# A two-layer conv and expert kernel: the layer norms shared by ScalarE and GpSimd, with new instruction orders

## The chip, the cores and the metric

The kernel runs on one core of a Trainium2 chip. A core has TensorE (PE in the profile; PEld is its weight load), VectorE (DVE), ScalarE (ACT), GpSimd (POOL) and SyncE (SP), each with its own instruction stream, held together by semaphores. The metric is the device time in microseconds of one execution; the median of three runs is given.

## The reference, cut to what matters

The input is x of 16 x 16 x 8 x 64 (height, width, image, channel). Two layers follow one another, and each has a convolution-like half and an expert half, both with a layer norm in front and a residual behind:

```
x = x + L0_conv(ln(x, 1e-6))      # projections, gates, four linear scans, norm, projection
t = x as 8 x 256 tokens
t = t + L0_ffn(ln(t, 1e-5))       # 16 experts, silu(h1) * h2, the two best weighted
x = x + L1_conv(ln(x, 1e-6))
t = t + L1_ffn(ln(t, 1e-5))       # 8 experts, gelu, the two best weighted
ln(v, eps) = (v - mean(v)) / sqrt(var(v) + eps)      # over the 64 channels
```

What is touched here is `ln` alone: two norms a layer, each over all 2048 rows of 64 channels.

## The kernel before

The rows lie in SBUF as 16 tiles of 128 rows by 64 channels. The work is cut into nine units (`UNITS`): in layer 0 two of one image (two tiles, 256 columns) and three of two images (four tiles, 512 columns), in layer 1 four of two images. Each unit goes through the same stages, and the stages of several units overlap.

A norm exists twice per unit, "a" ahead of the conv half and "e" (the token norm) ahead of the experts, so there are 18: 4 of two tiles, 14 of four. Each runs: DVE takes statistics (`a0`/`e0`), aggregates them (`a1`/`e1`) and adds eps (`a2`/`e2`, tile `spread`); POOL raises that to the power -0.5 (`ra`/`re`, tile `rstd`) and then subtracts the mean and multiplies by `rstd`, one `tensor_scalar` instruction for each tile (`an`/`en`, L599); PE transposes two tiles at a time (`TA`/`TE`, L1152); ACT and DVE split the result into a high and a low part (`za`/`al` and `ze`/`el`, tiles `conv_z` and `tok_z`), which the products read.

In the expert half PE makes two up products per expert (`U`, L1148 and L1149), ACT applies silu (`si`) or gelu (`ga`, `gb`), in layer 0 DVE multiplies (`hd`), PE makes the down product of two experts (`D`, L1263), DVE weighs it with the gates (`wp`), and POOL adds it up (`ad`, L664). The gates of a unit come from DVE and POOL (`sh`, ending in tile `gates`), are turned on PE, written to DRAM by ACT's queue and read back by SP's queue, broadcast to all partitions (`gates_b`).

The order on each engine is written out by hand, in five tables of short names (`PE_ORDER`, `DVE_ORDER`, `ACT_ORDER`, `POOL_ORDER`, `SP_ORDER`). An engine executes its table strictly in order; an instruction that waits for a semaphore holds all behind it. In `PE_ORDER` a name carries the PSUM bank and what must have freed it.

`NORM_BY` says which engine makes a unit's norm ("P" is POOL). Code for "S" (ACT) and "V" (DVE) is there and not used before; the "S" form is `Identity(rstd * x + shift)` with `shift = -mean * rstd`, for which DVE makes `minus_mean` (L948) and POOL the product (L588).

Of the kernel before, what the change touches and what calls it, by code (L numbers as in the profile page):

```python
# [4 lines left out]
H, W, B, D = 16, 16, 8, 64  # L5
# [23 lines left out]
NORM_BY = {"a": "PPPPPPPPP", "e": "PPPPPPPPP"}  # L29
# [19 lines left out]
D:3hd54 D:5al5 I:4wp23 F:2si55 XT:0si56 U:1hd55:6y4 U:7hd56:3wp24 U:5wp25:1si57 U:6hd57:7si58 TE:0x2 D:3hd58
U:5si59:1hd59 LG:6si60 U:0el4:7hd60 mx:5si61 U:3wp26:6lg4 D:1hd61 U:0si62:3si63 U:7hd62:6hd63 U:5mc1:1wp27  # L50
GT:0si64 D:7si65 D:5si66 D:0gt4 D:3hd64 U:2sc5:4sc5 TA:7wp28 O:5wp29 U:2si67:6hd65 U:1hd66:4hd67 GB:5og5 I:2si68
U:1si69:7al6 U:0wp30:6hd68 F:4hd69 U:1si70:3wp31 D:7hd70 D:0si71 D:5y5 D:1si72 XT:6hd71 U:3hd72:7wp32
U:0wp33:5wp34 U:3si73:1wp35 U:6x3:0si74 TE:7hd73 U:3si75:5hd74 U:1hd75:6si76 D:3si77 D:1si78 U:0hd76:5hd77
U:7el5:3wp36 LG:0si79 D:1wp37 U:6hd78:0lg5 O:7ga0 U:3gb0:6ga1 TA:0gb1 U:2sc6:4sc6 D:5hd79 I:3ga2 F:1wp38
U:6gb2:0al7 GB:2ga3 XT:4gb3 U:5wp39:7og6 GT:0gb4 O:6ga4 U:4x4:5ga5 U:7gb5:0gt5 D:2y6 D:4ga6 TE:7ga7 TA:5gb6
D:0gb7 LG:1sc7 U:3sc7:7el6 U:5al8:1lg6 U:3ga8:2wp40 U:7gb8:5ga9 GB:1gb9 I:6og7 U:3ga10:4wp41 F:2gb10 GT:5gb11
D:0wp42 D:7ga11 D:5gt6 U:3ga12:1y7 U:4gb12:0wp43 O:3ga13 TE:1gb13 D:4ga14 U:2sc8:6sc8 U:0gb14:1el7 U:7wp44:2ga15
LG:5wp45 GB:6gb15 U:0ga16:3og8 U:7ga17:1gb16 U:5lg7:2gb17 U:0ga18:3gb18 D:1gb19 U:6y8:2gb20 GT:3gb21
U:7ga19:4wp46 TE:2gb22 D:3gt7 D:5ga20 LG:0ga21 U:2el8:4gb23 U:6ga22:7ga23 XT:0lg8 U:2ga24:1wp47 U:4gb24:6ga25
GT:2ga26 D:7gb25 D:2gt8 D:3wp48 XT:4ga27 U:5wp49:1gb26 U:7wp50:2wp51 U:0x5:5ga28 U:6gb27:7ga29 D:1gb28 D:2gb29  # L60
D:0ga30 XT:3wp52 XT:5gb30
"""
# [90 lines left out]
def normed(n, engine):  # L153

    return [u for u in range(len(UNITS)) if NORM_BY[n][u] == engine]

# [1148 lines left out]
```

## Time and profile before

| | us |
|---|---|
| median of three runs | 245.09 (244.55 to 245.18) |
| the profiled execution | 243.74 |
| span of its instructions | 241.9 |
| busy PE / DVE / POOL / ACT | 208.1 / 185.9 / 177.5 / 153.4 |

All rows come from the profiled execution. Times count from the start of its span. A row of the timeline is a merged run of like instructions: start, duration, engine, line, operation, tiles, count, and in brackets how long the engine sat idle before it and what ended that. The granted clock of TensorE is 0.971 of full over the span.

### The profile page before, as it was taken

The page shows a single profiled execution, that of the slowest core. Times are in us where ns is not written, and L with a number is a line of the kernel's source. Part 1 is how long each engine was busy: PE and PEld are TensorE (multiplying, and loading weights), DVE is VectorE, ACT ScalarE, POOL GpSimd, SP SyncE. Part 2 cuts the span into 40 slices and gives each one's busy share as a digit, 9 for nine tenths or more (in the row PEclk, how much of TensorE's full clock was granted, in tenths as well). Part 3 has the DMA queues.
Part 4 walks back from the last instruction along what each step waited for, and adds up shares of the span by engine and source line. Part 5 has one row for each costly group of instructions (what it writes and reads, how often), then busy time and mean ns, then how long its engine had stood idle before and what let it go on. Part 6 is the DMA issues. An engine that isn't in the chain of part 4 may idle for free.

```text
span 241.9 us, 3831 instructions
## 1 busy us (share of the span) xinstructions
PE 208.1 (86%) x993; PEld 132.7 (55%) x993; DVE 185.9 (77%) x583; ACT 153.4 (63%) x358; POOL 177.5 (73%) x246
## 2 busy tenths in 40 slices
PE   0695787995999969999799996989969989999992
PEld 0483775784768635375463843646438338445531
DVE  2689798897689969999899879879966694435243
ACT  3593686587139756383592794589859889576440
POOL 5649989799859439975889779798894195847432
PEclk9999798999599999999999999999999999999999
DMA  3694005709604910195001940000240250052801
GB/s 105 153 223 66 1 4 143 137 29 196 129 0 109 214 34 0 48 213 97 0 0 58 210 88 1 0 0 0 79 100 0 69 111 3 0 137 42 193 26 43
DMA packets 19857, 18.52 MB, mean 77 GB/s; under 512 B 5350, under 2 KB 14716, under 8 KB 19836
## 3 DMA queue, kind: packets, MB, share of 16 engines
q1 hardware_dynamic: 19400, 18.08, 34.1%
q10 hardware_dynamic: 436, 0.20, 0.3%
q8 instruction: 8, 0.13, 0.2%
q14 instruction: 13, 0.11, 0.2%
HBM read 17.56 MB, written 0.72 MB: 76 GB/s over the span
## 4 chain that ended last, share of the span: by engine, by line
POOL 36%; PE 21%; DMA 17%; issue 14%; DVE 6%; ACT 2%; POOLq 1%; SPq 1%; DVEq 0%; ACTq 0%
DMA gates_b<-gates_dram 13%; POOL total L664 10%; PE bank L1263 8%; POOL norm_a L599 6%; POOL norm_e L599 6%; PE bank L1148 5%; PE bank L1149 4%; POOL rstd_e L585 3%; POOL rstd_a L585 3%; DMA gates_dram<-gates_t 3%; PE bank L1152 2%; POOL rstd_b L585 2%; DVE weighted L1107 2%; POOL gated L631 1%; POOL fwd_h L629 1%
## 5 line engine op out<-in xcount | busy, mean ns | idle before, releaser
L1148 PE MATMUL bank<-tok_z,up_hi 128*128 128x512 f32 (+1 forms) x224 | 86.5, 393 | 2.9 <-DVE tok_z L973 1.6
L1149 PE MATMUL bank<-tok_z,up_lo 128*128 128x512 f32 (+1 forms) x224 | 81.5, 370 | 0.0
L1263 PE MATMUL bank<-hidden,down 128*64 128x512 f32 (+1 forms) x288 | 61.8, 566 | 0.0
L664 POOL TENSOR_TENSOR total<-total,weighted 128x512 f32<-128x512 f32 (+1 forms) x47 | 52.6, 1120 | 12.0 <-DVE weighted L1110 7.9
L818 ACT ACTIVATE silu_h<-bank 128x512 f32<-128x512 f32 (+1 forms) x80 | 39.9, 513 | 33.4 <-PE bank L1149 28.9
L1148 PEld LDWEIGHTS bank<-tok_z,up_hi 128*128 128x128 f32 x224 | 44.2, 197 | 22.4 <-issue 9.6
L836 ACT ACTIVATE hidden<-bank,expert_bias 128x512 f32<-128x512 f32 x64 | 39.9, 694 | 13.5 <-PE bank L1149 11.2
L1149 PEld LDWEIGHTS bank<-tok_z,up_lo 128*128 128x128 f32 x224 | 44.1, 197 | 5.9
L1088 DVE TENSOR_TENSOR hidden<-silu_h,bank 128x512 f32<-128x512 f32 (+1 forms) x80 | 43.7, 569 | 1.3 <-PE bank L1149 0.4
L1263 PEld LDWEIGHTS bank<-hidden,down 128*64 128x64 f32 x288 | 19.0, 140 | 29.3 <-issue 23.0
L1107 DVE TENSOR_TENSOR weighted<-bank,gates_b 128x512 f32<-128x512 f32 (+1 forms) x35 | 19.5, 575 | 1.3 <-PE bank L1263 1.1
L599 POOL TENSOR_SCALAR norm_a<-rows,moments_a,rstd_a 128x64 f32<-128x64 f32 x32 | 19.2, 614 | 0.5
L599 POOL TENSOR_SCALAR norm_e<-rows,moments_e,rstd_e 128x64 f32<-128x64 f32 x32 | 18.2, 584 | 0.8
L585 POOL TENSOR_TENSOR rstd_e<-spread_e,minus_half 128x4 f32<-128x4 f32 (+1 forms) x9 | 8.5, 947 | 13.7 <-DVE spread_e L949 13.6
L616 POOL TENSOR_TENSOR up_lo<-up_raw,up_hi 128x512 fp32r<-128x512 f32 x11 | 14.0, 1279 | 2.3 <-ACT up_hi L696 2.3
L1152 PE MATMUL bank<-ident,norm_a 128*128 128x128 f32 x16 | 4.3, 345 | 12.7 <-POOL norm_a L599 11.5
L585 POOL TENSOR_TENSOR rstd_a<-spread_a,minus_half 128x4 f32<-128x4 f32 (+1 forms) x9 | 8.6, 958 | 7.5 <-DVE spread_a L949 7.1
L1148 PE MATMUL bank<-conv_z,in_hi 128*128 128x512 f32 (+1 forms) x27 | 12.5, 463 | 1.3 <-DVE conv_z L973 0.9
L973 DVE TENSOR_TENSOR tok_z<-bank,tok_z 64x256 fp32r<-64x256 f32 (+1 forms) x18 | 7.1, 393 | 8.5 <-ACT tok_z L791 8.2
L791 ACT ACTIVATE tok_z<-bank 64x256 fp32r<-64x256 f32 (+1 forms) x18 | 6.4, 354 | 10.2 <-PE bank L1152 10.1
L1152 PE MATMUL bank<-ident,norm_e 128*128 128x128 f32 x16 | 3.7, 302 | 10.1 <-POOL norm_e L599 10.1
L1110 DVE SCALAR_TENSOR_TENSOR weighted<-bank,expert_bias,gates_b 128x512 f32<-128x512 f32 x12 | 8.9, 744 | 4.2 <-PE bank L1263 4.2
(119 smaller groups left out, 357.0 us busy)
## 6 DMA issues: line engine op xcount, KB each, us to landing
gates_b<-gates_dram SPq DMA_DIRECT2D x12, 512.0 KB, 6.3
gates_b<-gates_dram SPq DMA_DIRECT2D x6, 1024.0 KB, 9.8
up_raw<-in_L_ffn_w_dram SPq DMA_DIRECT2D x8, 192.0 KB, 4.5
up_raw<-in_L_ffn_W_dram SPq DMA_DIRECT2D x2, 512.0 KB, 10.8
up_raw<-in_L_ffn_w_dram SPq DMA_DIRECT2D x4, 128.0 KB, 2.8
down<-in_L_ffn_w_dram SPq DMA_DIRECT2D x1, 512.0 KB, 7.6
down<-in_L_ffn_W_dram SPq DMA_DIRECT2D x1, 512.0 KB, 7.2
out_dram<-rows SPq DMA_DIRECT2D x4, 128.0 KB, 1.8
```

Source lines behind the costliest of these rows:

```text
L585: last = nc.gpsimd.tensor_tensor(rstd[n][:, 0:t], spread[n][:, 0:t], minus_half[:, 0:t], ALU.pow)
L599: last = nc.gpsimd.tensor_scalar(norm[n][:, i, :], row_tile(u, i), moments[n][:, i, 0:1], rstd[n][:, i:i + 1], ALU.subtract, ALU.mult)
L616: nc.gpsimd.tensor_tensor(lo, raw, hi.bitcast(fp32), ALU.subtract).then_inc(s_lo_pool, 1)
L664: nc.gpsimd.tensor_tensor(t, t, weighted[:, n % WEIGHTED, 0:c], ALU.add).then_inc(s_sum, 1)
L818: nc.scalar.activation(silu_h[:, n % SILUS, 0:c], bank("U", m)[:, 0:c], ACT.Silu).then_inc(s_silu, 1)
L836: nc.scalar.activation(hidden_of(n, j), bank("U", n, j)[:, 0:columns_of(u)], ACT.Gelu, bias=expert_bias[:, 2 * s + j:2 * s + j + 1]).then_ ...
L1088: nc.vector.tensor_tensor(hidden_of(m), silu_h[:, n % SILUS, 0:c], bank("U", m, 1)[:, 0:c], ALU.mult).then_inc(s_hid0, 1)
L1107: nc.vector.tensor_tensor(dst, product, g, ALU.mult).then_inc(s_pm, 1)
L1148: nc.tensor.matmul(dst, hi, z, start=True, stop=False)
L1149: return nc.tensor.matmul(dst, lo, z, start=False, stop=True)
L1152: return nc.tensor.transpose(dst, src, ident[0:k, 0:k])
L1263: last = nc.tensor.matmul(t[k * D:(k + 1) * D, 0:c], w, hidden_of(first + k, j), start=(j == 0), stop=(j == l))
```

## The change

`NORM_BY` now names two engines for each unit, "SP". ACT makes the first half of a unit's tiles with one `activation` per tile (scale `rstd`, bias `shift`), POOL the second half with two `tensor_tensor` instructions over all its tiles, a subtraction of the mean and a multiplication by `rstd`, each with an operand that is repeated along the channels. `shift` and `minus_mean` are made for every unit. The semaphore of a norm is split by engine, and who waited for it (PE's transpose, POOL's next `rstd`, the constant added to the rows) now waits for both.

```diff
-NORM_BY = {"a": "PPPPPPPPP", "e": "PPPPPPPPP"}
+NORM_BY = {"a": "SP SP SP SP SP SP SP SP SP".split(), "e": "SP SP SP SP SP SP SP SP SP".split()}
...
+def norm_tiles(n, u, engine):
+    share = tiles_of(u) // len(NORM_BY[n][u])
+    first = NORM_BY[n][u].index(engine) * share
+    return first, first + share
...
-        s_norm = {n: sem(f"normalised_{n}") for n in "ae"}
+        s_norm = {n: {e: sem(f"normalised_{n}_by_{e}") for e in "PSV"} for n in "ae"}
...
-                    if n != "b" and NORM_BY[n][u] == "S":
+                    if n != "b" and "S" in NORM_BY[n][u]:
                         link(last)
                         last = nc.gpsimd.tensor_tensor(shift[n][:, 0:t], minus_mean[n][:, 0:t], rstd[n][:, 0:t], ALU.mult)
...
-                    for i in range(tiles_of(u)):
-                        last = nc.gpsimd.tensor_scalar(norm[n][:, i, :], row_tile(u, i), moments[n][:, i, 0:1],
-                                                       rstd[n][:, i:i + 1], ALU.subtract, ALU.mult)
-                    last.then_inc(s_norm[n], 1)
+                    first, end = norm_tiles(n, u, "P")
...
+                    link(nc.gpsimd.tensor_tensor(centred, r, mean, ALU.subtract))
+                    nc.gpsimd.tensor_tensor(t, t, rstd[n][:, first:end].unsqueeze(2).broadcast_to([P, end - first, D]),
+                                            ALU.mult).then_inc(s_norm[n]["P"], 1)
...
-                    for i in range(tiles_of(u)):
+                    for i in range(*norm_tiles(n, u, "S")):
                         last = nc.scalar.activation(norm[n][:, i, :], row_tile(u, i), ACT.Identity,
                                                     bias=shift[n][:, i:i + 1], scale=rstd[n][:, i:i + 1])
...
 SP_ORDER = """
-gates in1 gates up1 gates gates gates gates gates gates gates store store store store
+in1 gates gates up1 gates gates gates gates gates gates gates store store store store
```

`link` makes an instruction signal and lets POOL wait for that signal before the next one. All five order tables are new; the other four share hardly a line with those of before. Three places show what moved.

**POOL and ACT at the token norm of the third unit.** On POOL, before: four additions into `total`, then `rstd` and the four tiles.

```order
L664 TENSOR_TENSOR total<-total,weighted 128x256 [waits pair_added,pair_weighted] x4
L585 TENSOR_TENSOR rstd_e<-spread_e,minus_half 128x4 [waits normalised_e,spread_ready_e]
L599 TENSOR_SCALAR norm_e<-rows,moments_e,rstd_e 128x64 [waits norm_turned_e,rstd_ready_e]
L599 TENSOR_SCALAR norm_e<-rows,moments_e,rstd_e 128x64 x3
L609 TENSOR_TENSOR rows<-rows,out_const 128x2x2x64
```

And now on POOL:

```order
L630 TENSOR_TENSOR rows<-rows,out_const 128x2x2x64 [waits normalised_a_by_P,normalised_a_by_S]
L685 TENSOR_TENSOR total<-total,weighted 128x256 [waits pair_added,pair_weighted]
L599 TENSOR_TENSOR rstd_e<-spread_e,minus_half 128x4 [waits normalised_e_by_P,normalised_e_by_S,spread_ready_e]
L602 TENSOR_TENSOR shift_e<-minus_mean_e,rstd_e 128x4 [waits pool_chain]
L620 TENSOR_TENSOR norm_e<-rows,moments_e 128x128 [waits norm_turned_e,rstd_ready_e]
L621 TENSOR_TENSOR norm_e<-norm_e,rstd_e 128x128 [waits pool_chain]
L685 TENSOR_TENSOR total<-total,weighted 128x256 [waits pair_added,pair_weighted]
```

And now on ACT, where before only silus stood around this place:

```order
L839 ACTIVATE silu_h<-bank 128x256 [waits hidden_ready0_by_vector,up_first_bank]
L726 ACTIVATE norm_e<-rows,shift_e,rstd_e 128x64 [waits rstd_ready_e]
L726 ACTIVATE norm_e<-rows,shift_e,rstd_e 128x64
L839 ACTIVATE silu_h<-bank 128x256 [waits hidden_ready0_by_vector,up_first_bank] x2
L812 ACTIVATE tok_z<-bank 64x2x128 [waits logits_product,up_second_bank,norm_turned_e]
```

The four tiles of POOL have become a short product and two passes over two tiles, the additions no longer stand in a block ahead of them, and ACT has two instructions more, which wait for POOL, ahead of the next silus.

**SP's queue after the loads at the start.** Before, with the gates of the first unit ahead of the weights of layer 1 (`in_raw`, `down`):

```order
L503 DMA expert_rows<-in_L_ffn_b_dram 4x128
L521 DMA gates_b<-gates_dram 64x8x256 [waits gates_sent0]
L521 DMA gates_b<-gates_dram 64x8x256
L477 DMA in_raw<-in_L_conv_in_w_dram 64x192 x2
L507 DMA down<-in_L_ffn_W_dram 128x16x64
L521 DMA gates_b<-gates_dram 64x8x256 [waits gates_sent1]
```

And now:

```order
L517 DMA expert_rows<-in_L_ffn_b_dram 4x128
L491 DMA in_raw<-in_L_conv_in_w_dram 64x192 x2
L521 DMA down<-in_L_ffn_W_dram 128x16x64
L535 DMA gates_b<-gates_dram 64x8x256 [waits gates_sent0]
L535 DMA gates_b<-gates_dram 64x8x256
L535 DMA gates_b<-gates_dram 64x8x256 [waits gates_sent1]
```

The weights of layer 1 no longer wait for the first gates; they follow the first loads.

**POOL at the start, the second unit's conv norm.** Before:

```order
L563 TENSOR_SCALAR over_t<-ident 64x32x2
L585 TENSOR_TENSOR rstd_a<-spread_a,minus_half 128x2 [waits normalised_a,spread_ready_a]
L599 TENSOR_SCALAR norm_a<-rows,moments_a,rstd_a 128x64 [waits norm_turned_a,rstd_ready_a]
L599 TENSOR_SCALAR norm_a<-rows,moments_a,rstd_a 128x64
L623 TENSOR_TENSOR gated<-fwd_w,rev_w 128x256 [waits row_scans_done]
L616 TENSOR_TENSOR up_lo<-up_raw,up_hi 128x512 [waits up_loaded0,up_high_parts]
```

And now:

```order
L577 TENSOR_SCALAR over_t<-ident 64x32x2
L637 TENSOR_TENSOR up_lo<-up_raw,up_hi 128x512 [waits up_loaded0,up_high_parts]
L599 TENSOR_TENSOR rstd_a<-spread_a,minus_half 128x2 [waits normalised_a_by_P,normalised_a_by_S,spread_ready_a]
L602 TENSOR_TENSOR shift_a<-minus_mean_a,rstd_a 128x2 [waits pool_chain]
L620 TENSOR_TENSOR norm_a<-rows,moments_a 128x64 [waits norm_turned_a,rstd_ready_a]
L621 TENSOR_TENSOR norm_a<-norm_a,rstd_a 128x64 [waits pool_chain]
L644 TENSOR_TENSOR gated<-fwd_w,rev_w 128x256 [waits row_scans_done]
```

The low part of the first expert weights (`up_lo`, `ul` in the table) now stands ahead of this norm; on ACT the two roundings that it needs (`up_hi`, `uh`) stand ahead of the first unit's `tanh_f`.

## Rows read from the trace of the kernel before

**Rows 1.** The head of the page: span, and DVE's busy tenths in 40 slices.

```profile
span 241.9 us, 3831 instructions
...
DVE  2689798897689969999899879879966694435243
```

**Rows 2.** The waits: engine, line, releaser, us in total, times, longest.

```profile
PE bank L1152 <- POOL norm_a L599: 11.5, 5, 6.2
...
PE bank L1152 <- POOL norm_e L599: 10.1, 8, 2.5
```

**Rows 3.** PE's timeline: four of the ten transposes after 24 us that waited.

```profile
26.76 0.69 PE L1152 MATMUL bank<-ident,norm_a 128*128 128x128 f32 x2 [1.26 <-POOL norm_a L599]
...
59.11 0.44 PE L1152 MATMUL bank<-ident,norm_e 128*128 128x128 f32 x2 [2.52 <-POOL norm_e L599]
...
196.84 0.44 PE L1152 MATMUL bank<-ident,norm_e 128*128 128x128 f32 x2 [0.79 <-POOL norm_e L599]
...
212.05 0.44 PE L1152 MATMUL bank<-ident,norm_e 128*128 128x128 f32 x2 [0.80 <-POOL norm_e L599]
```

**Rows 4.** POOL's timeline at the third unit's token norm.

```profile
55.65 1.02 POOL L585 TENSOR_TENSOR rstd_e<-spread_e,minus_half 128x4 f32<-128x4 f32 x1 [0.20 <-DVE spread_e L949]
56.78 2.27 POOL L599 TENSOR_SCALAR norm_e<-rows,moments_e,rstd_e 128x64 f32<-128x64 f32 x4
```

**Rows 5.** Groups by shape: count, busy us, mean ns of one, idle before.

```profile
L599 POOL TENSOR_SCALAR norm_a<-rows,moments_a,rstd_a 128x64 f32<-128x64 f32 x32 | 19.2, 614 | 0.5
...
L599 POOL TENSOR_SCALAR norm_e<-rows,moments_e,rstd_e 128x64 f32<-128x64 f32 x32 | 18.2, 584 | 0.8
...
L767 ACT ACTIVATE bank<-bank 128x64 f32<-128x64 f32 x32 | 6.8, 235 | 0.4 <-PE bank L1217 0.3
...
L949 DVE TENSOR_SCALAR spread_a<-moments_a 128x4 f32<-128x4 f32 x7 | 1.9, 273 | 0.1
...
L641 POOL TENSOR_TENSOR pick<-pick,shares 128x64 f32<-128x64 f32 x6 | 1.8, 298 | 2.6 <-DVE pick L1079 2.3
...
L641 POOL TENSOR_TENSOR pick<-pick,shares 128x128 f32<-128x128 f32 x3 | 1.2, 408 | 0.3
...
L949 DVE TENSOR_SCALAR spread_e<-moments_e 128x4 f32<-128x4 f32 x7 | 1.1, 164 | 0.1
...
L609 POOL TENSOR_TENSOR rows<-rows,out_const 128x128 f32<-128x128 f32 x2 | 0.9, 458 | 0.0
```

**Rows 6.** The chain that ended last, 36 to 60 us: start, duration, what.

```profile
37.37 8.34 DMA gates_b<-gates_dram
...
48.22 0.21 POOL spread_b L577
48.42 0.07 issue
```

**Rows 7.** Stretches: length; PE, PEld, DVE, ACT, POOL busy (count); clock; DMA; GB/s.

```profile
54.00:60.00 6.00, 3.48 (x29) 2.90 (x29) 5.14 (x11) 4.58 (x11) 5.55 (x9) 1.00 0.90 190
60.00:66.00 6.00, 6.00 (x32) 4.42 (x29) 3.71 (x15) 1.12 (x3) 5.13 (x8) 0.55 0.78 149
96.00:102.00 6.00, 5.66 (x24) 2.40 (x22) 6.00 (x7) 1.99 (x4) 5.84 (x10) 1.00 0.02 7
```

**Rows 8.** SP's queue beside the first gates, and the page's DMA issues.

```profile
38.05 2.49 SPq L477 DMA_DIRECT2D in_raw<-in_L_conv_in_w_dram  x2
...
gates_b<-gates_dram SPq DMA_DIRECT2D x12, 512.0 KB, 6.3
```

**Rows 9.** The start: ACT's first tanh_f and POOL's first up_lo.

```profile
8.80 0.47 ACT L726 ACTIVATE tanh_f<-bank,half_bias 128x256 f32<-128x256 f32 x1 [1.51 <-PE bank L1149]
...
14.83 1.27 POOL L616 TENSOR_TENSOR up_lo<-up_raw,up_hi 128x512 fp32r<-128x512 f32 x1 [2.16 <-ACT up_hi L696]
```

**Rows 10.** The waits once more: ACT's longest.

```profile
ACT silu_h L818 <- PE bank L1149: 28.9, 30, 4.3
```

More of the change, by code:

```diff
@@ L62 @@
+U:7ga16:1lg7 GB:4ga17 D:3og8 GT:6gb16 U:2gb17:7ga18 U:0wp44:6gt7 XT:5wp45 U:2ga19:3wp46 D:0ga20 D:4y8 D:2ga21
+TE:1gb18 U:7gb19:0wp47 U:6gb20:5x5 LG:3gb21 U:1el8:0gb22 U:4wp48:7ga22 U:2wp49:5gb23 XT:3lg8 U:6ga23:1ga24
+GT:4ga25 D:0gb24 D:2ga26 U:7gb25:4gt8 U:5gb26:6ga27 U:0wp50:2wp51 U:7ga28:1gb27 D:4gb28 D:6gb29 D:5ga29 D:2gb30
+XT:0ga30 XT:7ga31
 """
 DVE_ORDER = """
[L64 to L65 removed]
@@ L153, in normed @@
 def normed(n, engine):
-    return [u for u in range(len(UNITS)) if NORM_BY[n][u] == engine]
+    return [u for u in range(len(UNITS)) if engine in NORM_BY[n][u]]
+def norm_tiles(n, u, engine):
+    share = tiles_of(u) // len(NORM_BY[n][u])
+    first = NORM_BY[n][u].index(engine) * share
+    return first, first + share
 def by_pool_before(n):
@@ L412, in turned_low, with wait_norm @@
             return z[r, :].rearrange("p (m k n) -> p m k n", k=2, n=P)[:, :, k, :]
+        def wait_norm(eng, n, u, by="PSV"):
+            for e in NORM_BY[n][u]:
+                if e in by:
+                    eng.wait_ge(s_norm[n][e], normed(n, e).index(u) + 1)
         def unit_rows(u):
@@ L703, in make @@
                         act.wait_ge(s_turn[n], u)
-                    for i in range(tiles_of(u)):
+                    for i in range(*norm_tiles(n, u, "S")):
                         last = nc.scalar.activation(norm[n][:, i, :], row_tile(u, i), ACT.Identity,
                                                     bias=shift[n][:, i:i + 1], scale=rstd[n][:, i:i + 1])
-                    last.then_inc(s_norm[n], 1)
+                    last.then_inc(s_norm[n]["S"], 1)
                 return make
@@ L925, in make @@
                         dve.wait_ge(s_conv, u + 1)
+                    if u:
+                        dve.wait_ge(s_moments[n], u)
                     for k in range(t):
@@ L933, in make @@
                     dve.wait_ge(s_stats[n], u + 1)
-                    if u and NORM_BY[n][u - 1] != "S":
-                        dve.wait_ge(s_norm[n], u)
+                    if u:
+                        wait_norm(dve, n, u - 1, "PV")
                     for k in range(tiles_of(u)):
@@ L958, in make @@
                         dve.wait_ge(s_turn[n], u)
-                    for i in range(tiles_of(u)):
+                    for i in range(*norm_tiles(n, u, "V")):
                         last = nc.vector.tensor_scalar(norm[n][:, i, :], row_tile(u, i), moments[n][:, i, 0:1],
                                                        rstd[n][:, i:i + 1], ALU.subtract, ALU.mult)
-                    last.then_inc(s_norm[n], 1)
+                    last.then_inc(s_norm[n]["V"], 1)
                 return make
```

102 lines of the change are left out of this document (53 added, 49 removed).

## Prediction

> **What bounds the kernel now.** I read the page's busy shares first. PE is the busiest engine, 208.1 of 241.9 us, so at most some 34 us can be won by closing its gaps; the question is who opens them. The list of waits answers it: PE's transposes waited 11.5 us in 5 places for norm_a and 10.1 us in 8 for norm_e, both from POOL [rows 2]. That is 21.6 of the 34 us. PE's own timeline then says where. Three of the thirteen lie in the first 24 us, where the pipeline fills; the other ten come to 13.0 us, the first at 26.76, the last at 212.05, the shortest 0.79 and the longest 2.52 [rows 3]. Before each of them POOL does the same thing: rstd in 1.02 us and then four tiles in 2.27 us [rows 4]. So a four-tile norm on POOL ends last at ten places, and whatever shortens it shortens PE's gap there, up to the point where another engine is late.
>
> The stretches show who that other engine would be. At 96 to 102 DVE is busy 6.00 of 6.00 and POOL 5.84, with PE at 5.66 [rows 7]; DVE has 15 slices of 40 at nine tenths or more [rows 1]. So PE, DVE and POOL are all close to full in the middle, and a gain on POOL alone will not arrive whole.
>
> **The change part by part.**
>
> *POOL's half of a norm.* Removed: the four instructions, 2.27 us [rows 4], 584 to 614 ns each [rows 5]. Added behind rstd: the small product for shift and two passes over 128 x 128. No row has this very pass, but two have two inputs at this size: 408 ns, with one operand repeated along the innermost axis just as here, and 458 ns [rows 5]. I take 0.43, the middle, with 0.41 and 0.46 as ends. For the 128x4 product the nearest is POOL's 0.21 us on a tile of that size, and the gap of a linked pair is 0.07 us [rows 6]. So the new tail is 0.07 + 0.21 + 0.07 + 0.43 + 0.07 + 0.43 = 1.28 us against 2.27: about 1.0 less. For the two-tile units it is 0.07 + 0.21 + 0.07 + 0.30 + 0.07 + 0.30 = 1.02 (298 ns at 128 x 64) against 2 x 0.58 = 1.17 [rows 5]; I count nothing there.
>
> What speaks against this part is a rule. The rows say that one tensor_scalar on 64 columns with two per-row operands costs 584 to 614 ns, more than a two-input pass over twice as many columns [rows 5]. The Trainium skill (GPSIMD Engine Reference, section 4.1 "Engine selection", with 3.1) has it the other way: one-input work on GpSimd runs at roughly line rate and two-input work at about 2.6 cycles an element, so that two two-input passes for one one-input pass would be a loss; by that, the added passes would cost about 0.28 us each plus a fixed part (an estimate from that page), and the removed ones should have been cheap. The trace does not agree for the form that is removed, and the row decides.
>
> *DVE's minus_mean.* One more 128x4 instruction ahead of each spread, 18 in all: 164 to 273 ns by its neighbour [rows 5], I take 0.2. It lies on the way to rstd, so each norm gains 1.0 - 0.2 = 0.8 us net (0.7 to 0.85 between the ends).
>
> *ACT's half.* 32 instructions on 64 columns, 235 ns by the nearest row [rows 5], 7.5 us together on an engine that is busy 153 us and waits 28.9 us for PE in silu alone [rows 10]. Two take 0.47 us and start when POOL starts its first pass, so they are covered by POOL's 0.93, if ACT is there in time. If it is not, PE's transpose waits for ACT; and if it is there too early, the silus queued behind its wait stand still (third rival).
>
> *The sum at the ten places.* Each wait is 0.79 us or longer, so each can give its 0.8: 8.0 us. That is the upper end; the lower end is nothing, where DVE or PSUM banks end the gap instead. I take half, 4.0, because DVE and PE themselves are near full in the middle, and because one of the ten stands in the clear: only at the third unit's token norm is PE's gap, and not DVE, the plain mark of its stretch (PE 3.48 of 6.00, DVE 5.14 at 54 to 60 [rows 7]).
>
> *SP's order.* The first gates broadcast stands on the chain that ended last with 8.34 us [rows 6]; the median landing of that size is 6.3, and right behind it SP issued layer 1's weights, which share the DMA engines [rows 8]. With those moved to the front, where SP would only have waited, up to 2.0 us is saved at this one place; I count 1.0, as the gates themselves may come earlier or later in the new POOL order. The moved loads fall into a part of the start that has its own loads (the rest of x and the first down weights), but nothing in layer 0 reads them.
>
> *The start.* Two roundings (0.6 us each) now precede ACT's first tanh_f; before it ACT was idle for 1.51 us [rows 9], which covers them if the weights have landed. Behind them POOL's up_lo (1.27 us), which waited 2.16 us for ACT at its old place [rows 9], now precedes the second unit's norm. The first unit waits for the second only where DVE's queue puts the second unit's low part ahead of the first's sum. Between 0 and 1.3 us lost; I take 0.4.
>
> *The rest of the order.* The block of four additions no longer stands ahead of the third unit's token norm on POOL, and DVE's e1 and e2 stand closer behind e0 there. This is part of how the gap at 59.11 would close; I do not count it again.
>
> *Sum.* -4.0 - 1.0 + 0.4 = -4.6 us. On the profiled execution: span 241.9 to 237.3, and with the 1.8 around it 243.7 to 239.1. The median stands 1.35 above that execution, so 245.1 becomes **240.5**; a spread of 238 to 243.5 belongs to this case.
>
> **The rivals.**
>
> 1. *It arrives whole.* All ten waits give 0.8 (-8.0), the broadcast its 2.0, the start costs 0.4, and the clock comes back in part: after the 2.52 us wait the granted clock is 0.55 over 60 to 66, that is mostly the lower of its two levels, which for that stretch costs 0.45 x 6 = 2.7 us of full speed [rows 7]; with a shorter wait I count half, 1.3. 245.1 - 8.0 - 2.0 - 1.3 + 0.4 = 234.2, around **234.5**. For it: at all ten places it is POOL that ends last. Against it: DVE's 6.00 of 6.00 [rows 7].
>
> 2. *DVE is the floor.* The ten waits turn into waits for DVE and give nothing; minus_mean adds 18 x 0.2 = 3.6 us, which counts in the 15 of 40 slices where DVE is full, 1.35 us. 245.1 - 1.0 + 0.4 + 1.35 = **245.8**. For it: 6.00 of 6.00 at 96 to 102; against it: in the stretch with the largest gap DVE is at 5.14 and after it at 3.71 [rows 7].
>
> 3. *ACT stands still in front of the norm (slower).* ACT now waits for POOL's rstd and shift with silus or gelus queued behind, and PE's next up product needs the bank that such a silu frees. If ACT arrives when POOL begins rstd, it stands for 1.02 + 0.28 = 1.3 us [rows 4, 6]. With h as the mean hold at the 14 four-tile norms and half of it reaching PE, the end moves by -4.6 + 7h: it decides from h = 0.66 us. At h = 1.1 it is +3.1, **248**. For it: ACT had no wait of this kind on its way before. Against it: ACT waits 28.9 us for PE in silu [rows 10], that is it is usually early with nothing to do, and such a hold is then free.
>
> 4. *The passes cost more than the form they replace (slower).* If two-input passes over rows with a repeated mean cost per column what the old form did (0.57 a tile), a pass is 1.14 and the tail 2 x 1.14 + 0.42 = 2.70, with DVE's 0.2 a loss of 0.6 at each of ten places, half of it 3.1: 245.1 - 0.6 + 3.1 = **247.6**. This is the sign that the GPSIMD page's rule (the Trainium skill) gives, by another road. Both rows at this size speak against it.
>
> **How the numbers follow.** Forecast 0.50, whole 0.21, DVE 0.13, ACT 0.13, passes 0.03. About 0.3%, 0.74 us, is what a measurement here can tell from no change. The forecast and the first rival are faster; of the DVE case I put 0.02 under 244.4, 0.08 within and 0.03 above 245.8; the last two are slower. Faster 0.73, same 0.08, slower 0.19. The range 234.5 to 247 leaves out the better half of the first rival and half or so of the two slow ones, under 0.2 together.
>
> **What would show it.** Right: POOL's two passes at 0.41 to 0.46 us and its busy time down by some 19 us (37.4 out [rows 5], 14 x 1.07 + 4 x 0.81 = 18.2 in); the waits of the transposes for norm_a and norm_e down from 21.6 to about 14 us; first gates landed well before 45 us and in 6 us or less. First rival: no low granted clock between 50 and 72 us. Second: PE's gaps released by DVE (tok_z, conv_z) instead of POOL. Third: ACT idle on its norm lines, released by POOL, and PE waits on silu or gelu grown. Wrong altogether: passes of 0.6 us or more, or a start in which the first expert product comes later than before by more than a microsecond.

## The result, and the profile after

The changed kernel takes **232.78 us** (median of four runs, 232.45 to 235.14) beside 244.82 for the one before in the same group: a ratio of 0.956, with a 95% interval of 0.945 to 0.966. The prediction was 240.5 us with a range of 234.5 to 247.0. The direction was right and the size was not: 12.0 us were gained, not 4.6, and the time lies below the range. The profiled execution is one of 232.45 us, with a span of 230.3 and a mean granted clock of 0.995; the other three have 0.971 to 0.980, and the profile before has 0.971.

The page's head after: span, busy time of each engine, DVE's tenths, the granted clock, and the shares of the chain that ended last.

```profile
span 230.3 us, 3867 instructions
...
PE 203.3 (88%) x993; PEld 127.5 (55%) x993; DVE 186.0 (81%) x601; ACT 164.2 (71%) x390; POOL 158.8 (69%) x236
...
DVE  2778999899799979999999999999948947453144
...
PEclk9999999999999999999999999999999999999998
...
PE 38%; DVE 25%; issue 11%; DMA 11%; POOL 6%; ACT 5%; SPq 2%; POOLq 1%; DVEq 0%; ACTq 0%
```

PE's busy time fell from 208.1 to 203.3 us and its idle time from 33.8 to 27.0, so of the 11.6 us of span 6.8 are idle time and 4.8 busy time, at a clock of 0.995 in place of 0.971. DVE's busy time is the same (186 us). DVE had 15 slices of 40 at nine tenths or more [rows 1] and has 23. POOL lost 18.7 us of work, as the prediction had it, and has 6% of the chain.

The waits after (engine, line, releaser; total, times, longest):

```profile
PE bank L1175 <- POOL norm_a L621: 5.8, 1, 5.8
PE bank L1175 <- ACT norm_e L726: 4.4, 4, 2.3
PE bank L1171 <- DVE conv_z L996: 3.8, 3, 1.7
```

PE's transposes waited 21.6 us for norms before [rows 2], now 10.4 (with 0.2 for ACT's norm_a). After 24 us there were ten waits of 13.0 us [rows 3]; now there are four of 3.3 us, all behind ACT's half. Three of the four lie at old places (1.0 us in sum), so the ten gave 12.0 us. The fourth and longest, at 37.55, is new: it is the second unit's token norm, for which PE did not wait before. PE's timeline:

```profile
26.79 0.41 PE L1175 MATMUL bank<-ident,norm_a 128*128 128x128 f32 x2 [0.20 <-ACT norm_a L726]
...
37.55 0.33 PE L1175 MATMUL bank<-ident,norm_e 128*128 128x128 f32 x1 [2.25 <-ACT norm_e L726]
...
54.05 0.41 PE L1175 MATMUL bank<-ident,norm_e 128*128 128x128 f32 x2 [0.26 <-ACT norm_e L726]
...
108.97 0.41 PE L1175 MATMUL bank<-ident,norm_e 128*128 128x128 f32 x2 [0.57 <-ACT norm_e L726]
```

POOL's timeline at the third unit's token norm, the place of [rows 4]:

```profile
51.69 1.02 POOL L599 TENSOR_TENSOR rstd_e<-spread_e,minus_half 128x4 f32<-128x4 f32 x1 [1.19 <-DVE spread_e L972]
52.78 0.20 POOL L602 TENSOR_TENSOR shift_e<-minus_mean_e,rstd_e 128x4 f32<-128x4 f32 x1
53.07 0.40 POOL L620 TENSOR_TENSOR norm_e<-rows,moments_e 128x128 f32<-128x128 f32 x1
53.55 0.40 POOL L621 TENSOR_TENSOR norm_e<-norm_e,rstd_e 128x128 f32<-128x128 f32 x1
```

From the end of rstd (52.71) to the end of the norm (53.95) it is 1.24 us. Before it was 2.38, from 56.67 to 59.05 [rows 4]: the 2.27 of the four tiles and the gap of 0.11 ahead of them. The groups by shape (count, busy us, mean ns) answer to [rows 5]:

```profile
L726 ACT ACTIVATE norm_e<-rows,shift_e,rstd_e 128x64 f32<-128x64 f32 x16 | 6.3, 435 | 3.4 <-POOL shift_e L602 3.2
...
L620 POOL TENSOR_TENSOR norm_e<-rows,moments_e 128x128 f32<-128x128 f32 x7 | 2.8, 402 | 0.5
...
L971 DVE TENSOR_SCALAR minus_mean_e<-moments_e 128x4 f32<-128x4 f32 x7 | 1.1, 164 | 0.1
```

And the stretches of [rows 7] (length; PE, PEld, DVE, ACT, POOL busy; clock; DMA; GB/s):

```profile
54.00:60.00 6.00, 5.71 (x42) 4.38 (x44) 5.17 (x26) 4.21 (x12) 5.41 (x9) 1.00 0.97 187
60.00:66.00 6.00, 5.34 (x33) 3.07 (x30) 4.85 (x11) 4.17 (x9) 3.40 (x8) 1.00 0.61 121
96.00:102.00 6.00, 5.42 (x28) 3.48 (x27) 5.89 (x22) 3.51 (x15) 4.07 (x8) 1.00 0.00 0
```

PE's 3.48 of 6.00 at 54 to 60 became 5.71, and the granted clock of 0.55 behind it became 1.00. It is 1.00 there in the two later profiles of this kernel too, but they have low stretches elsewhere; in the one of the fourth group below (mean clock 0.979) the clock was 0.60 around the new wait:

```profile
36.00:42.00 6.00, 4.08 (x17) 2.41 (x18) 5.25 (x9) 3.56 (x11) 5.38 (x6) 0.60 0.44 108
```

Over the middle, in the same columns, DVE now has hardly a gap:

```profile
84.00:156.00 72.00, 67.28 (x302) 40.90 (x300) 71.10 (x184) 51.23 (x112) 56.83 (x67) 1.00 0.28 60
```

Before it was busy for 65.20 of these 72 us.

### The profile page after: what moved, and what is told of

It reads as the page before. It is cut to its first block, busy times and chain, and to the rows that moved or that the text cites. A ratio compares the mean times of both kernels' runs of the same rounds, so it can differ in the third digit from the quotient of the medians.

```text
span 230.3 us, 3867 instructions
## 1 busy us (share of the span) xinstructions
PE 203.3 (88%) x993; PEld 127.5 (55%) x993; DVE 186.0 (81%) x601; ACT 164.2 (71%) x390; POOL 158.8 (69%) x236
## 4 chain that ended last, share of the span: by engine, by line
PE 38%; DVE 25%; issue 11%; DMA 11%; POOL 6%; ACT 5%; SPq 2%; POOLq 1%; DVEq 0%; ACTq 0%
PE bank L1286 13%; PE bank L1171 10%; PE bank L1172 8%; DMA gates_b<-gates_dram 8%; DVE hidden L1111 5%; DVE weighted L1130 3%; PE bank L1175 2%; PE bank L1240 2%; POOL total L685 2%; DMA gates_dram<-gates_t 2%; DVE fwd_w L1024 1%; DMA up_raw<-in_L_ffn_w_dram 1%; DVE rev_h L1025 1%; DVE tok_z L996 1%; DVE rows L1051 1%
## 5 line engine op out<-in xcount | busy, mean ns | idle before, releaser
L1171 PE MATMUL bank<-tok_z,up_hi 128*128 128x512 f32 (+1 forms) x224 | 84.6, 386 | 2.8 <-DVE tok_z L996 1.6
L1172 PE MATMUL bank<-tok_z,up_lo 128*128 128x512 f32 (+1 forms) x224 | 79.4, 363 | 0.0
L839 ACT ACTIVATE silu_h<-bank 128x512 f32<-128x512 f32 (+1 forms) x80 | 39.8, 514 | 27.4 <-PE bank L1172 21.9
L1171 PEld LDWEIGHTS bank<-tok_z,up_hi 128*128 128x128 f32 x224 | 42.1, 188 | 21.2 <-issue 8.1
L1172 PEld LDWEIGHTS bank<-tok_z,up_lo 128*128 128x128 f32 x224 | 42.2, 189 | 5.5
L1286 PEld LDWEIGHTS bank<-hidden,down 128*64 128x64 f32 x288 | 18.2, 136 | 32.3 <-issue 25.5
L652 POOL TENSOR_TENSOR gated<-gated,fwd_h 128x512 f32<-128x512 f32 x7 | 10.8, 1548 | 0.5
L1171 PEld LDWEIGHTS bank<-conv_z,in_hi 128*128 128x128 f32 x27 | 5.7, 209 | 9.7 <-DVE conv_z L996 6.0
L650 POOL TENSOR_TENSOR fwd_h<-fwd_h,rev_h 128x512 f32<-128x512 f32 x7 | 9.0, 1286 | 2.4 <-DVE rev_h L1025 2.4
L1172 PE MATMUL bank<-conv_z,in_lo 128*128 128x512 f32 (+1 forms) x27 | 10.7, 395 | 0.0
L644 POOL TENSOR_TENSOR gated<-fwd_w,rev_w 128x512 f32<-128x512 f32 (+1 forms) x9 | 10.4, 1155 | 0.1
## 6 DMA issues: line engine op xcount, KB each, us to landing
up_raw<-in_L_ffn_W_dram SPq DMA_DIRECT2D x2, 512.0 KB, 11.9
```

Source lines behind the costliest of these rows:

```text
L644: nc.gpsimd.tensor_tensor(gated[:, 0:c], fwd_w[:, 0:c], rev_w[:, 0:c], ALU.add).then_inc(s_sum_w, 1)
L652: nc.gpsimd.tensor_tensor(square(gated, u), square(gated, u), turned(fwd_h, u), ALU.add).then_inc(s_sum_h, 1)
L839: nc.scalar.activation(silu_h[:, n % SILUS, 0:c], bank("U", m)[:, 0:c], ACT.Silu).then_inc(s_silu, 1)
L1171: nc.tensor.matmul(dst, hi, z, start=True, stop=False)
L1172: return nc.tensor.matmul(dst, lo, z, start=False, stop=True)
L1286: last = nc.tensor.matmul(t[k * D:(k + 1) * D, 0:c], w, hidden_of(first + k, j), start=(j == 0), stop=(j == l))
```

## The experiments

Four parts came together in the change: a cheaper form of the norm on GpSimd, a second engine for half of it, new orders on four engines, and a new order of SP's transfers. And the prediction had halved the gain. The runs came in four groups, each on one chip with the kernel before beside it; only within a group do differences of 1 to 2 us mean anything. The diffs are shortened to the lines that matter.

### The form alone, the orders alone

In the first group, **two passes, old orders**: POOL does all four tiles in two instructions and ACT has no part. In the diff, `mean` and `rstd_over_columns` stand for the values of each row, repeated along the channels.

```diff
-for i in range(tiles_of(u)):
-    last = nc.gpsimd.tensor_scalar(norm[n][:, i, :], row_tile(u, i), moments[n][:, i, 0:1],
-                                   rstd[n][:, i:i + 1], ALU.subtract, ALU.mult)
+link(nc.gpsimd.tensor_tensor(centred, r, mean, ALU.subtract))            # four tiles, 128x256
+nc.gpsimd.tensor_tensor(t, t, rstd_over_columns, ALU.mult)               # in place
```

> Every order of work as before, SP's too; only the form of the norm changes: GpSimd does all four tiles of a norm in two instructions over 128x256 (subtract the mean, multiply by rstd) where it did four tensor_scalars of 584 to 614 ns; ScalarE has no part in it. An estimate from the changed kernel's 400 ns at 128x128 and before's 298 ns at 128x64: some 0.6 us a pass, so 1.3 us in place of 2.27. Theory N (the shorter norm, with the clock that returns when the gaps close, makes most of the 12 us): 235 to 239 us, and PE's waits for norm_a and norm_e fall from 21.6 to about 12 us. Theory O (the new orders make most of it): 242 to 245 us, the waits come back as waits for other engines.

Measured: 233.37 us beside 243.53, ratio 0.956 (0.952 to 0.960). This edit alone, in the old orders, gives 10.2 us, most of the gain, and comes out under theory N's range. Its waits, PE's timeline at all the waits for norms that are left after 24 us, and the page's clock row:

```profile
PE bank L1174 <- POOL norm_a L620: 6.8, 3, 5.7
PE bank L1174 <- POOL norm_e L620: 2.9, 4, 1.5
```

```profile
57.35 0.44 PE L1174 MATMUL bank<-ident,norm_e 128*128 128x128 f32 x2 [1.53 <-POOL norm_e L620]
...
115.22 0.44 PE L1174 MATMUL bank<-ident,norm_e 128*128 128x128 f32 x2 [0.36 <-POOL norm_e L620]
...
146.19 0.44 PE L1174 MATMUL bank<-ident,norm_e 128*128 128x128 f32 x2 [0.70 <-POOL norm_e L620]
...
170.82 0.44 PE L1174 MATMUL bank<-ident,norm_a 128*128 128x128 f32 x2 [0.17 <-POOL norm_a L620]
```

```profile
PEclk9999785799999997999999999999999999999998
```

The ten waits of 13.0 us have become four of 2.8, and the three at the start went from 8.6 to 6.9. So 11.9 us of waits are gone; PE's idle time fell by 9.8 (33.8 to 24.0), the span by 8.9 (241.9 to 233.0) and the median by 10.2. In this profiled execution the mean granted clock is 0.960, lower than the 0.971 of the profile before, and PE's busy time is 209.0 beside 208.1, so these 8.9 us are not from the clock. Each pass over 128x256 took 614 to 656 ns in the mean, 1.3 us for a norm.

**Old norm, new orders**: the changed kernel with POOL's four tensor_scalars back, and ACT's entries left out of its order.

```diff
-NORM_BY = {"a": "SP SP SP SP SP SP SP SP SP".split(), "e": "SP SP SP SP SP SP SP SP SP".split()}
+NORM_BY = {"a": "PPPPPPPPP", "e": "PPPPPPPPP"}                           # and tensor_scalar as before
```

> All five orders as changed, but the norm as before: GpSimd alone, four tensor_scalars a unit, no shift, no minus_mean, and ScalarE's entries for the norm left out of its order. Theory N: 242 to 246 us, with waits of PE for the norms of 15 us or more and low granted clock in some stretches. Theory O: 233 to 237 us. If both parts are needed together (each order fits only its own norm): above 238 us here and in the run with the old orders and the two passes.

Measured: 237.39 us, ratio 0.971 (0.966 to 0.977), just above theory O's range, while the two passes alone had come out under theory N's: the orders alone do about half of what the whole does. The waits for norms:

```profile
PE bank L1168 <- POOL norm_a L613: 8.6, 3, 6.4
PE bank L1168 <- POOL norm_e L613: 7.5, 5, 2.8
```

16.1 us in place of 21.6. The orders close some of the same waits, with the norm as slow as it was; that PE has other work there when a norm is late is how I read it, and not shown place by place. They also make the new wait: at 39.53, the second unit's token norm, it is 2.85 us here.

**The changed norm in the old orders.** ACT's entries were put where POOL began that norm in the trace of before.

```diff
-an ih za uh uh tf vi lw ca cl an to za ...        # the changed kernel's ACT order
+an ih za tf vi an lw ca cl za mc uh to ...        # the old one, with an and en set in by time
```

> The changed norm whole (GpSimd's two passes over half of the tiles, ScalarE the other half, with minus_mean and shift), in the old orders of all engines; ScalarE's share stands in its order where, by the trace of before, GpSimd began that norm. Theory N: 234 to 238 us, close to the changed kernel's 232.8. Theory O: 242 us or more. A third view, that ScalarE stands still in front of the norm unless its order is made for it: ScalarE's idle time on the norm's line 8 us or more and 240 us or more.

Measured: 240.22 us, ratio 0.980 (0.973 to 0.987); three of the four executions took 237.86 to 240.38, one 245.46 at a mean clock of 0.843. It is nearest to the third view: ACT's idle time is beyond its 8 us, and the time is at its edge, with an interval that reaches into theory N's range. ACT's waits:

```profile
ACT norm_a L726 <- POOL shift_a L602: 5.1, 5, 2.9
ACT norm_e L726 <- POOL shift_e L602: 4.1, 3, 2.0
```

ACT stood 9.2 us in front of its halves (6.0 in the changed kernel), and the kernel is slower than with POOL alone in the same orders, by 5.7 us by the ratios and 6.9 by the medians, with intervals that don't touch. The places were mine, so this shows that sharing can lose, and not that it must in these orders.

**Two passes, new orders**: the changed kernel without the sharing.

> All five orders as changed, GpSimd does the whole norm in two passes over 128x256, ScalarE has none of it (its entries left out), no shift and no minus_mean. It differs from the changed kernel by the sharing alone. If the sharing is what counts: 236 us or more, with PE's waits for norms back on GpSimd. If the cheaper form is what counts: 231 to 234 us, since the second half costs GpSimd about 0.2 us a pass, and DVE and ScalarE are spared 18 and 32 instructions.

Measured here: 230.67 us, ratio 0.945 (0.941 to 0.949). But the same kernel beside the changed one, in the third group, stood elsewhere:

> The changed kernel as it is, beside the three others of this group. 232 to 234 us.

> The new orders with the whole norm by GpSimd in two passes, as it is, beside the changed kernel: 230 to 231.5 us, 1.5 to 2.5 us under it, if the sharing is worth less than nothing; within 0.7 us of it if the two groups of runs differed by chip only.

Measured: 233.10 for the changed kernel and 232.47 without the sharing, ratios 0.958 and 0.957. These medians do not confirm a 2 us loss by the sharing, and the whole square was run once more, on one chip.

> Old orders, norm by GpSimd in two passes, now beside the three others on one chip. 233 to 234.5 us. If the new orders give nothing beyond the two passes, the run with the new orders and the two passes lies within 0.7 us of it; if they give what the first group showed, 2.7 us under it.

> New orders, norm as before. In the first group 6.1 us under the kernel before. If the orders and the passes close the same waits: 236.5 to 238.5 us here, and together they give far less than the sum of both (10 and 6). If that was chip alone: 240 us or more.

> New orders, whole norm by GpSimd in two passes. 230.5 to 232.5 us.

> The changed kernel as it is. If the sharing is worth nothing: within 0.7 us of the run with the new orders and GpSimd alone. If it costs what the first group showed: 2 us over it.

| Fourth group, us (ratio to before, 95% interval) | old orders | new orders |
|---|---|---|
| norm as before | 243.62 | 237.34 (0.969 to 0.980) |
| GpSimd alone, two passes | 232.91 (0.953 to 0.965) | 232.08 (0.945 to 0.958) |
| shared with ScalarE, the changed kernel | | 233.29 (0.954 to 0.965) |

The passes alone give 10.7 us and the orders alone 6.3, but both together 11.5, not 17: they close the same waits. On top of the passes the orders give 0.8 us and the sharing -1.2, neither of which these intervals tell from nothing.

The granted clock of each execution tells more. The time of one and the same kernel goes with it: the 46 executions of the kernel before have a median of 244.2 us at a mean clock of 0.960 to 0.966, 243.0 at 0.976 to 0.981 and 241.7 at 0.983 to 0.987. The kernel with two passes and new orders took 229.53, 230.97 and 231.13 us at 0.985 and 0.986, in three groups; the changed kernel took 232.32 to 233.57 in five executions at 0.983 to 0.985. So at like clocks the sharing costs some 1.5 us (an estimate from these executions; the clock was not set by any run, and the sharing may itself move it). The 230.67 of the first group came at clocks of 0.974 to 0.993, the 232.47 of the third at 0.974 to 0.985; at like clocks the two agree (232.14 and 232.40 at 0.974, 230.97 and 231.13 at 0.985).

The four orders were not tried apart, other than SP's: each engine's new order waits for places of the others', and a mixture of old and new ones could deadlock.

### How much of a microsecond arrives

**Three passes**: two passes and old orders, with the first pass issued twice.

```diff
 link(nc.gpsimd.tensor_tensor(centred, r, mean, ALU.subtract))
+link(nc.gpsimd.tensor_tensor(centred, r, mean, ALU.subtract))
```

> The kernel with the old orders and the two passes by GpSimd, with the first pass issued twice: each four-tile norm ends some 0.7 us later (a pass of 617 to 656 ns and the 0.07 of a link), nothing else moves. It asks how much of a microsecond at the norm's end reaches the kernel's end. That kernel stood 10.2 us under the one before for 0.96 us a norm, as much as 10.6 norms that give all. Theory 'whole' (PE's waits give and take in full): +0.7 x 10.6 = 7.4, about 240 to 241.5 us. Theory 'half' (what the prediction took: other engines take up the other half): +3 to 4 us, 236.5 to 237.5.

Measured: 240.95 us, ratio 0.988 (0.984 to 0.993), beside 0.956 for the same without the third pass: 7.6 us by the medians, 7.8 by the ratios, for 0.7 us at each norm (7.2 by the ratio of the same kernel in the fourth group). It lies in the range of 'whole', 4 us above that of 'half'. The waits are back, and PE's timeline at two of them:

```profile
PE bank L1175 <- POOL norm_a L621: 10.9, 5, 6.3
PE bank L1175 <- POOL norm_e L621: 8.6, 8, 2.2
```

```profile
59.44 0.44 PE L1175 MATMUL bank<-ident,norm_e 128*128 128x128 f32 x2 [2.23 <-POOL norm_e L621]
...
116.32 0.44 PE L1175 MATMUL bank<-ident,norm_e 128*128 128x128 f32 x2 [1.06 <-POOL norm_e L621]
```

1.53 became 2.23 and 0.36 became 1.06, each by the 0.7. After 24 us there are ten waits again, 10.2 us in sum: 7.4 more than without the third pass, and about what the kernel lost. With the three waits at the start, which grew from 6.9 to 9.3, it is 9.8 us of waits, of which PE's idle time shows 7.1 (24.0 to 31.1) and the kernel 7.6. So about three quarters or more of what PE waits for a norm arrives.

### SP's order alone

The kernel before, with SP's new order and nothing else.

```diff
-gates in1 gates up1 gates gates gates gates gates gates gates store store store store
+in1 gates gates up1 gates gates gates gates gates gates gates store store store store
```

> The kernel before with SP's new order and nothing else: layer 1's in-weights and down-weights are issued ahead of the first gates broadcast. The prediction's step counts 1.0 us of gain, 2.0 at most (broadcast 8.34 to 6.3 us). Against it: in the changed kernel the broadcast still took 7.96 us with nothing of SP's behind it; then the broadcast is no shorter here either, and the time is that of before within 0.7 us.

Measured: 243.57 beside 244.14, ratio 1.000 (0.997 to 1.004). No gain that this interval shows. The first broadcast is issued in two parts. With layer 1's weights gone from behind them, the two took, from issue to landing, first here and then before (min is the first part, max the second):

```profile
DMA to landing us min/median/max: 5.8/6.7/7.5
...
DMA to landing us min/median/max: 5.4/6.9/8.3
```

So the later part landed 0.8 us sooner after its issue, 7.5 in place of 8.34, about what the prediction counted. The longer of the two took 7.7 to 8.5 us in the five profiles with SP's old order, and 7.2 to 8.0 in the thirteen with the new one. But it did not arrive. In this execution the issue came 0.6 us later, so that the part landed at 45.5 beside 45.7. Over the four parts from 25 to 62 us the median is 7.1 here and 7.0 before.

### What the sharing puts in the way, and how full DVE is

**Shift and minus_mean made and not used**, on two passes and new orders (the same `if` goes ahead of minus_mean on DVE); the next edit is in the same kernel, **a copy on DVE** behind each spread.

```diff
-if n != "b" and "S" in NORM_BY[n][u]:             # shift, on GpSimd
+if n != "b":
```

```diff
+link(nc.vector.tensor_copy(spare[:, :], moments[n][:, 0, 1:2].broadcast_to([P, 2 * D])))
```

> The kernel with the new orders and the whole norm by GpSimd in two passes, plus minus_mean on DVE and shift on GpSimd, which nobody reads: of the sharing, what stands ahead of the norm, without ScalarE's part. Per norm 0.17 and 0.20 to 0.26 and a link of 0.07, about 0.45 to 0.5 us later. If the sharing loses its 2 us by these steps: 233 to 236 us. If it loses them by ScalarE itself (12.6 us more work, norms that come late behind silus): 230.5 to 231.5.

> The kernel with the new orders and the whole norm by GpSimd in two passes, with one copy of 128x128 on DVE behind each of the 18 spreads, off the way to the norm (about 0.25 us with its link, 4.5 us in all, an estimate from the 0.2 to 0.27 us of DVE's small instructions). If DVE is the floor of the whole: +3 to 4.5 us, 234 to 235. If it is the floor only in layer 0's middle: +1 to 2.5. If DVE's fullness costs nothing: 230.7 within 0.7.

Measured: 234.91 (ratio 0.961, 0.955 to 0.966) and 235.28 (0.966, 0.961 to 0.971). The same kernel without either stood at 0.945, 0.957 and 0.952 in the three other groups, so by the ratios the first cost 1 to 4 us and the second 2 to 5, and the ratio alone fixes no more. At like clocks (0.971 to 0.974) the first took 234.78 to 236.27 us, and the kernel without it 232.14 and 232.40; the second took 235.47 and 233.81 at 0.971 and 0.972. In the trace of the first, PE's waits for norms rose from 8.3 to 12.5 us:

```profile
PE bank L1174 <- POOL norm_a L620: 7.3, 4, 6.2
PE bank L1174 <- POOL norm_e L620: 5.2, 5, 1.8
```

That is the tail that the sharing adds in front of a norm, 0.45 us by the rows, about what ACT then takes off POOL's passes (2 x 0.21). DVE's 4.0 us of copies (18 of 220 ns), which no norm waits for, seem to cost as well. That DVE has little room left would explain it; it was not shown by a run beside the same kernel without them.

**minus_mean by GpSimd** in the changed kernel, and **the subtraction ahead of rstd** in the kernel with two passes and new orders:

```diff
-nc.vector.tensor_scalar(minus_mean[n][:, 0:t], moments[n][:, 0:t, 0], -1.0, None, ALU.mult)
+nc.gpsimd.tensor_scalar(minus_mean[n][:, 0:t], moments[n][:, 0:t, 0], -1.0, None, ALU.mult)  # ahead of its wait for spread
```

```diff
 pool.wait_ge(s_moments[n], u + 1)
+link(nc.gpsimd.tensor_tensor(centred, r, mean, ALU.subtract))
 pool.wait_ge(s_spread[n], u + 1)
```

> The changed kernel with one thing moved: minus_mean is made by GpSimd while it waits for the spread, and no longer by DVE (18 instructions, 160 to 175 ns, 3.0 us, ahead of each spread). Copies of 4.0 us in all on DVE had cost about 4.6 us. If it is DVE's time by which the sharing loses to GpSimd alone: 2 to 3 us under the changed kernel. If it is ScalarE's late halves (PE waited 4.4 us for them in four places): within 0.7 us of the changed kernel, since GpSimd then starts its rstd no earlier.

> The same, with GpSimd's subtraction of the mean ahead of rstd instead of behind it: it needs only the moments, and GpSimd had waited for the spread (7 us for each norm's seven units). Each norm would end some 0.25 us sooner where GpSimd is idle (DVE's spread and its signal), so 1 to 2 us under the run beside it. Against it: the subtraction must wait until PE has read the tile of the unit before, now ahead of rstd, and where GpSimd had other work at that time it only swaps places: within 0.7 us.

Measured: 232.52 beside 233.10, and 231.65 beside 232.47. Both are inside what can be told from no change, and both point downwards. In the second POOL waits for the moments where it had waited for the spread:

```profile
POOL norm_a L606 <- DVE moments_a L964: 6.9, 3, 5.0
POOL norm_e L606 <- DVE moments_e L964: 4.8, 4, 2.0
```

In the run beside it POOL waited 8.8 and 7.0 us for spread_a and spread_e, and PE's transposes 8.5 us for norms; here the transposes wait 7.8. So the subtraction fits into idle time, and PE's waits are 0.7 us shorter. At like clocks it gains nothing that shows (231.43 us at 0.985, beside 230.97 and 231.13 without it). This is the fastest version of its group, 231.65 us at a ratio of 0.953 (0.949 to 0.957), and simpler than the changed kernel (0.958, 0.954 to 0.963); the intervals overlap, so that it beats it is likely and not shown.

## Why the prediction was wrong in size

**What bounds the kernel**: right. POOL's norm ended last at ten places, and closing those waits was most of the gain: they gave 12.0 us, the start 1.6, and the new wait at 37.55 took 2.25 back. Other gaps of PE grew, so that its idle time fell by 6.8 us only.

**POOL's tail**: right, and what it replaced was longer than counted. 1.28 us was worked out from the end of rstd, and 1.24 measured. The old tail, counted from there too, was 2.38 and not 2.27, so the norm's end moved by 1.14 and not by 1.0. A pass took 400 to 402 ns at 128x128, just under the 0.41 to 0.46 taken from neighbours. The removed form was the dear one, as its row said.

The Trainium skill (GPSIMD Engine Reference, section 3.1 "Elementwise — side-by-side cycle accounting") gives two-input work about 2.6 cycles an element, 2.2 ns at the 1.2 GHz it reckons with, an estimate. From 128x128 (401 ns) to 128x256 (614 to 656 ns) the rows here give 1.7 to 2.0 ns a column, so the trace is below the page.

**"I take half, 4.0"**: this is the step that failed. The ten places gave 12.0 us, and 10.2 of them with the cheaper form alone. The reason given was DVE's 6.00 of 6.00 at 96 to 102 and the full slices. But none of the ten waits lies in 96 to 102. In the run with two passes and old orders DVE is 6.00 of 6.00 in that very stretch, and the kernel is 10.2 us faster:

```profile
96.00:102.00 6.00, 6.00 (x26) 2.92 (x25) 6.00 (x9) 2.19 (x5) 5.22 (x4) 1.00 0.31 86
```

Behind eight of the ten waits DVE itself stood idle, for 0.30 to 4.81 us, until ACT had passed on what PE had transposed (tok_z or conv_z); at 86.72 it waited for gates_b, and only behind 175.90 was it not idle. DVE's timeline before, behind the waits at 59.11 and 178.13:

```profile
60.39 0.86 DVE L973 TENSOR_TENSOR tok_z<-bank,tok_z 64x256 fp32r<-64x256 f32 x2 [1.25 <-ACT tok_z L791]
...
179.40 0.86 DVE L973 TENSOR_TENSOR conv_z<-bank,conv_z 64x256 fp32r<-64x256 f32 x2 [1.28 <-ACT conv_z L716]
```

The 5.14 of DVE at 54 to 60 [rows 7], on which the halving leaned too, speaks for room at the one place that was looked at. The third pass then showed the exchange in the other direction: 7.4 us of waits at the ten places, 7.6 us of time.

**0.8 us as the most that a wait can give**: too little. The norm's end moved by 1.14 less the 0.17 of minus_mean, 0.97, and two norms in a row on POOL add up. POOL's and PE's timelines before:

```profile
173.57 2.27 POOL L599 TENSOR_SCALAR norm_e<-rows,moments_e,rstd_e 128x64 f32<-128x64 f32 x4
175.82 2.25 POOL L599 TENSOR_SCALAR norm_a<-rows,moments_a,rstd_a 128x64 f32<-128x64 f32 x4
...
178.13 0.44 PE L1152 MATMUL bank<-ident,norm_a 128*128 128x128 f32 x2 [1.79 <-POOL norm_a L599]
```

With two passes in the old orders 0.17 us of the 1.79 is left. At 59.11 the new orders helped: 2.52 became 0.26. The three waits of the first 24 us, which I counted at nothing, went from 8.6 to 7.1 us. So even 'whole' at 0.8 a place would have stayed above what was measured: 245.1 - 8.0 + 0.4 is 237.5.

**ACT's half**: mis-sized. 235 ns came from an ACTIVATE without per-row operands; with two it is 435 ns, 12.6 us in all and not 7.5. Two in a row take 0.77 to 0.79 us, just under POOL's passes of 0.40 + 0.07 + 0.40, so ACT covers its half only if it begins when POOL does. All four waits left after 24 us are ACT's. The longest has another cause than the size: POOL's part was done at 36.68, and ACT's stood behind two long instructions in ACT's order, of which this is the second:

```profile
36.12 1.05 ACT L765 ACTIVATE lam_rh<-tanh_f 128x480 f32<-128x480 f32 x1
37.04 0.46 ACT L726 ACTIVATE norm_e<-rows,shift_e,rstd_e 128x64 f32<-128x64 f32 x1
```

Without the sharing PE waits there too, for POOL, 1.0 to 1.4 us. The Trainium skill (ScalarE: Activation LUTs, section "What ACT_TABLE_LOAD costs") has 186 ns plus 0.833 a column plus 93 for each per-row operand. For 64 columns and two operands that is 425, an estimate that the trace agrees with at 435; it was there to be used.

**SP's order**: the -1.0 was wrong as a term of the sum. The landing did get shorter by about that, but alone it gave nothing. In the changed kernel the first broadcast takes 7.96 us, against 8.34 before [rows 6], and not 6.3. The row of the chain after:

```profile
32.81 7.96 DMA gates_b<-gates_dram
```

It lands at 40.8 where it had landed at 45.7, but since its issue came 4.6 us earlier. The median that I took for an undisturbed landing hid landings of 5 to 9 us; what spreads them stays open.

**The start**: +0.4 forecast, and +0.6 measured at the first expert product, 24.09 before and 24.71 after:

```profile
24.09 0.36 PE L1148 MATMUL bank<-tok_z,up_hi 128*128 128x256 f32 x1 [1.60 <-DVE tok_z L973]
...
24.71 0.36 PE L1171 MATMUL bank<-tok_z,up_hi 128*128 128x256 f32 x1 [1.55 <-DVE tok_z L996]
```

The roundings waited for their weights, and POOL's first up_lo then still waited 0.34 us for them, 2.16 before [rows 9]. The two parts of the change pull in opposite ways here: with the norm's form held, the new orders put PE's first token transpose 1.1 us later with the old norm (22.16 to 23.26) and 1.4 with two passes (21.03 to 22.42), and the cheaper form takes about as much off.

**"The rest of the order: I do not count it again"**: right in the net, since the orders give 0.8 us on top of the passes, which the intervals do not tell from nothing. That they are worth 6.3 us by themselves I had not seen.

**The clock**: the forecast had no term for it, and the first rival gave it 1.3 us. The changed kernel ran at mean clocks of 0.971 to 0.995 in its 16 executions, the kernel before at 0.944 to 0.986 in 46, half of them at 0.965 or less. At like clocks (0.976 to 0.981) the medians are 233.3 and 243.0 us. So some 9.7 us come at like clocks; the rest of the 12.0 goes with the clock and with the scatter of four executions. That the closed waits raised the clock is likely, since the 0.55 behind the wait at 59.11 is gone, and not shown by a run of its own.

**The rivals.** "It arrives whole" (234.5) was the case, with another sum: 12.0 in place of 8.0 from the ten waits, nothing from the broadcast, and some from the clock. "DVE is the floor" was refuted for the gain: PE's waits for conv_z grew from 0.9 to 3.8 us, and the ten places still gave 12.0 of their 13.0; it is nearer to the truth of the kernel after. "ACT stands still" was seen in the run with my own places for it, and in the changed kernel only at the start (longest waits 2.7 and 2.6 us, at 4.92 and 22.04); ACT's wait for PE in silu fell from 28.9 [rows 10] to 21.9 us. "The passes cost more" was refuted by 402 ns.

## What to carry to other kernels

Where the trace names the engine that ends last, place by place, take most of what each place gives (three quarters or more here); halve it only for another engine's wait that is seen at that same place, and not for an engine that is busy elsewhere in the program. Two changes that each close the same wait don't add up, so a change made of a cheaper form, a second engine and a new order is worth trying part by part: here one part did nearly all of it, and the sharing could be left out, at like clocks with a gain of some 1.5 us. Price an instruction by a row with the same kinds of operands, not only by one of the same size, and count the old and the new form from the same point.

## What was not expected of the hardware

- On GpSimd one tensor_scalar of 128x64 with two per-row operands takes 584 to 614 ns, as long as a two-input instruction over 128x256 (614 to 656 ns), and twice one over 128x64 (294 ns). Four tiles in one instruction cost 0.2 us more than two.
- The mean granted clock of an execution goes with its time, but does not settle it. Two executions of the changed kernel had the same span of 230.3 us at 0.979 and at 0.995; without the sharing, 0.974 and 0.992 went with 230.3 and 228.2. Where the clock fell in the executions without a trace is not on record.
- The same kernel's ratio to the one before differed by 1.2% between two groups of runs (0.945 and 0.957), with intervals that don't touch. It ran at a median clock of 0.989 in the one and 0.976 in the other, and at like clocks its times agree within 0.3 us. Differences of that size need both kernels side by side, and their clocks beside the times.
